# One add on GpSimd in place of one identity product on TensorE, ahead of each finish of an attention and expert layer

## The reference, cut to what matters

```python
x = x + _L0_xattn_ref(_layernorm(x), ctx, ctx, mask, wq, bq, wk, bk, wv, bv, wo, bo)
x = x + _L0_ffn_ref(_layernorm(x), ...)

# _L0_ffn_ref
scores = sigmoid(xf @ gate_w + bias)
top_scores, top_idx = top_k(scores, 2)           # two experts for each token
top_scores = top_scores / (sum(top_scores) + 1e-06)
combined = sum over the two experts of weight * 0.1 * expert(xf)
shared = (gelu(xf @ sw_up + sb_up) @ sw_down + sb_down) * 0.1
out = shared + combined
out = out / (max(abs(out), axis=-1, keepdims=True) + 1e-06)
```

## Time and profile before

| | |
|---|---|
| median of 3 runs | 904.52 us (900.25 to 906.15) |
| the profiled execution | 901.51 us, its span 899.8 us |
| TensorE busy | 819.6 us (91%) |
| VectorE busy | 640.1 us (71%) |
| ScalarE busy | 652.6 us (73%) |
| GpSimd busy | 533.0 us (59%) |
| mean granted clock of TensorE | 0.971 |

### The profile page before, as it was taken

The page is one execution under the profiler, slowest core; times in us unless marked ns, Lnnn a source line. Parts: engine busy times, 40 slices in busy tenths (PEclk is TensorE's granted clock), DMA queues, the critical chain, the costliest instruction groups (busy, mean ns, idle before and its releaser), DMA issues.

```text
span 899.8 us, 21793 instructions
## 1 busy us (share of the span) xinstructions
PE 819.6 (91%) x7037; PEld 552.8 (61%) x7037; DVE 640.1 (71%) x1768; ACT 652.6 (73%) x1184; POOL 533.0 (59%) x631
## 2 busy tenths in 40 slices
PE   0779999998989989999987889999999999999997
PEld 0335555554545545555555667787888888778664
DVE  4355768866768677875756786877777777777677
ACT  1357888887867858677679878987888887889420
POOL 6246555788796857858647772365666565665000
PEclk9889999999989989999989899999999999999999
DMA  5133343442442312222001145566677688851875
GB/s 163 60 110 101 95 129 105 136 126 84 141 134 65 87 42 78 68 63 70 29 13 39 62 158 194 216 232 245 251 245 254 233 294 270 281 198 50 230 209 171
DMA packets 101382, 128.84 MB, mean 143 GB/s; under 512 B 21143, under 2 KB 81367, under 8 KB 95255
## 3 DMA queue, kind: packets, MB, share of 16 engines
q1 hardware_dynamic: 92183, 108.04, 37.4%
q0 software_dynamic: 9088, 19.42, 6.2%
HBM read 78.79 MB, written 40.56 MB: 133 GB/s over the span
## 4 chain that ended last, share of the span: by engine, by line
PE 55%; POOL 20%; issue 11%; ACT 6%; DVE 5%; DMA 2%; SPq 0%; POOLq 0%; ACTq 0%; DVEq 0%
PE bank L1250 7%; POOL xs_scratch L1118 7%; POOL y_scratch L1125 7%; PE bank L1236 5%; ACT prob L708 4%; PE bank L1267 3%; PE bank L1343 3%; PE bank L1342 3%; PE bank L1341 3%; PE bank L1255 3%; PE bank L1330 3%; PE bank L1332 3%; PE bank L1331 3%; POOL prob L1103 2%; PE bank L1229 2%
## 5 line engine op out<-in xcount | busy, mean ns | idle before, releaser
L708 ACT ACTIVATE prob<-bank,padb,sc 120x512 f32<-120x512 f32 x256 | 178.3, 777 | 77.7 <-PE bank L1255 77.7
L1125 POOL DMA_INDIRECT y_scratch<-yo,ti x156 | 158.0, 1013 | 122.6 <-DVE yo L1038 86.6
L1103 POOL TENSOR_SCALAR_AFFINE_SELECT prob<-prob 120x512 f32<-120x512 f32 x256 | 158.6, 634 | 89.7 <-ACT prob L708 85.6
L814 DVE TENSOR_REDUCE nm<-bank 128x4 f32<-128x480 f32 x256 | 150.4, 649 | 80.6 <-PE bank L1236 80.1
L1017 DVE TENSOR_TENSOR gl<-gf,gh 128x512 fp32r<-128x512 f32 x220 | 150.2, 688 | 49.6 <-ACT gh L754 48.9
L1118 POOL DMA_INDIRECT xs_scratch<-x2r,idx x128 | 127.2, 994 | 34.8 <-issue 34.4
L754 ACT ACTIVATE gh<-gf 128x512 fp32r<-128x512 f32 x220 | 138.5, 630 | 5.1
L1250 PE MATMUL bank<-qblk,kT 32*120 32x512 f32 x512 | 111.7, 646 | 3.4 <-DVE nm L814 3.4
L749 ACT ACTIVATE gf<-bank,wt 128x512 f32<-128x512 f32 x156 | 105.9, 679 | 5.3 <-DVE gl L1017 5.1
L1267 PE MATMUL bank<-prob,vm 120*32 120x128 f32 x2048 | 72.8, 285 | 8.9 <-POOL prob L1103 8.8
L1236 PE MATMUL bank<-kblk,qT 32*128 32x480 f32 x512 | 74.0, 646 | 1.5 <-DMA kblk<-kT 1.5
(11 more groups left out here) (190 smaller groups left out, 1654.8 us busy)
## 6 DMA issues: line engine op xcount, KB each, us to landing
wt<-w_scratch SPq DMA_DIRECT2D x39, 1032.0 KB, 5.1
xt<-xs_scratch SPq DMA_DIRECT2D x39, 280.0 KB, 5.0
w_scratch<-x2t SPq DMA_DIRECT2D x8, 1024.0 KB, 5.1
xs_scratch<-padc SPq DMA_DIRECT2D x15, 280.0 KB, 3.0
x<-in_x SPq DMA_DIRECT2D x16, 256.0 KB, 2.9
qblk<-qT SPq DMA_DIRECT2D x64, 64.0 KB, 2.1
x_scratch<-x SPq DMA_DIRECT2D x16, 256.0 KB, 2.9
fx<-x_scratch SPq DMA_DIRECT2D x16, 256.0 KB, 5.4
```

The costliest lines, as they stand in the source:

```text
L708: e.activation(prob[u % NP][0:LK, :], banks[bi][0:LK, :], ACT.Exp, scale=sc[0:LK, 0:1], bias=padb[0:LK, t:t + 1]).then_inc(a_ex, 1)
L814: e.tensor_reduce(nm[:, g, i // 2, :], bk[:, 0:480].rearrange("p (j k) -> p j k", j=4), AX.X, ALU.max, negate=True).then_inc(v_mx, 1)
L1103: e.affine_select(out=pv, in_=pv, compare_op=ALU.is_ge, fill=0.0, base=0, pattern=[[0, 4], [1, 128]], channel_multiplier=-1).then_inc(p_cu ...
L1125: e.indirect_dma_start(y_dram, bass.IndirectOffsetOnAxis(ap=ti_[r % NWS][:, c:c + 1], axis=0), yo_[r % NYO][:, c, :], None).then_inc(d_y[r ...
```

## The change

A stage "fsum" is put into the plan, 2.2 ahead of the finish. In it GpSimd waits for both loads of routed results, adds `fb` to `fa` in place and counts up a new semaphore `p_fs`. TensorE's "sum" waits for `p_fs` where it waited for the loads, and has one identity product, by `fa`, in place of two.

```diff
         plan.append((load, len(plan), "f_load", f, 0))
+        plan.append((time - 2.2, len(plan), "fsum", f, 0))
         plan.append((time - .4, len(plan), "sum", f, 0))
...
+                elif stage == "fsum":
+                    e.wait_ge(d_f[n % NF], 32 * (n // NF + 1))
+                    e.tensor_tensor(fa_[n % NF][:, :, :], fa_[n % NF][:, :, :], fb_[n % NF][:, :, :], ALU.add).then_inc(p_fs, 1)
...
                     e.wait_ge(v_ye, FINS[n] + 1)
-                    e.wait_ge(d_f[n % NF], 32 * (n // NF + 1))
+                    e.wait_ge(p_fs, n + 1)
                     e.matmul(bk[:, :], ident, fa_[n % NF][:, :, :].rearrange("p b h -> p (b h)"), start=True, stop=False, skip_group_check=True)
-                    e.matmul(bk[:, :], ident, fb_[n % NF][:, :, :].rearrange("p b h -> p (b h)"), start=False, stop=False, skip_group_check=True)
                     for b in range(GB):
```

More of the change, by code:

```diff
@@ L471, in xattn_moe_kernel @@
         d_out = [sem(f"d_out{i}") for i in range(NFX)]
-        p_set, p_vz, p_kb, p_qb, p_rs1, p_rs2, p_xb, p_cut, p_wl = map(
-            sem, ("p_set", "p_vz", "p_kb", "p_qb", "p_rs1", "p_rs2", "p_xb", "p_cut", "p_wl"))
+        p_set, p_vz, p_kb, p_qb, p_rs1, p_rs2, p_xb, p_cut, p_wl, p_fs = map(
+            sem, ("p_set", "p_vz", "p_kb", "p_qb", "p_rs1", "p_rs2", "p_xb", "p_cut", "p_wl", "p_fs"))
         v_set, v_id, v_bob, v_km, v_vis, v_poi = map(sem, ("v_set", "v_id", "v_bob", "v_km", "v_vis", "v_poi"))
```

## The result

The changed kernel took 897.6 us (median of 22 runs, 892.4 to 904.1), the kernel before 901.7 us beside it (22 runs, 895.6 to 907.0). The ratio is 0.9957, 95% interval 0.9938 to 0.9977: 3.9 us faster, between 2.1 and 5.6. I had forecast 898 and a gain of 5.9, in a range that ran from 893.4 to 901.5 before it was rounded outwards.

A forecast was written before the change was run, and what follows sets the result against it. TensorE was taken to bound the last 60 us by a third of a microsecond per finish. Ceiling 8.1 us, cut by late loads to 5.9 (4.5 to 7 at 0.54): 895.6 or 898.6, given as 898; range 893.4 to 901.5, rounded outwards.

The forecast's parts named there:

- rival (b): Transfers slower than 2.55 us, or adds sometimes meeting the small TENSOR_SCALAR: 2.86 to 3.1 per step, gain 3 to 4.3; 0.14 shared.
- (d): TensorE's clock drops to 1.2 GHz, a sum then takes 3.5 us: 1 to 2 us lost; chance 0.14 shared.
- What bounds, and what the product is worth: TensorE bounds the last 60 us; one identity product less saves 0.86 us per sum, 2.61 to 1.75.
- The wait in front of sum 0: 1.3: At the start TensorE waits for GpSimd's first add, hidden by nothing: costs 1.3 us, bounds 1.1 and 1.6.
- Mixed half: Sums 0 to 7, among shared tiles' products: step 5.4 to 4.55 us, 5.6 us ahead at its end.
- VectorE's finish at 2.3: Sums 8 to 15: VectorE bounds at 2.3 us against 2.61, gaining 2.5; with the earlier sums a ceiling of 8.1.
- Load 10 late, by SyncE's own chain: SyncE's queue waits on output landings, so finish 10's loads land at about 872.7; one microsecond lost.
- Then finish 10 at 875.9: After load 10: 1.4 us for the add, 1.75 for the sum, 0.05, so finish 10 starts at 875.9.
- At 315 three transfers are 2.5 us ... I take 2.55.: Finishes 10 to 15: the queue's three transfers set 2.55 us per step, 12.8 in all, last finish at 888.7.
- The shared reads: GpSimd's add could hold the finish's small TENSOR_SCALAR; costed at nothing, up to 7.6 us for adds 10 to 15.
- Rival (a): VectorE is the bound and the loads are in time: gain 8.1 us, 893.4; chance 0.20.
- rival (c): Every GpSimd add holds VectorE fully, 1.27 us per finish: 8.5 us slower, 910.0; chance 0.05.

The follow-up runs named there:

- wait_only: Changed kernel with the second identity product put back on TensorE, keeping the wait and GpSimd's add; ratio to the kernel before 1.0036, tail 72.4 us.
- before_mates: Kernel before with late x loads one finish later, 1e-6 added with a PSUM operand, two buffers for maxima and reciprocals; ratio to it 0.9989, tail 69.2 us.
- late_fx: Changed kernel with the five late loads of x one finish later in SyncE's list, behind the next output; ratio to the kernel before 0.9963, tail 65.2 us.
- first_direct: Changed kernel with finish 0 done the old way, both products on TensorE, GpSimd adding from finish 1 on; ratio to the kernel before 0.9945, tail 65.3 us.
- late_and_first: Changed kernel with finish 0 done the old way and the late x loads one finish later; ratio to the kernel before 0.9943, tail 63.6 us.
- filler: Changed kernel with idle identity products on TensorE ahead of its waits in sums 0 (two) and 10 (three); ratio to the kernel before 0.9957, tail 65.4 us.
- combo: Changed kernel with finish 0 the old way, late x loads one finish later, 1e-6 with a PSUM operand, two buffers for maxima and reciprocals; ratio 0.9922, tail 59.9 us.
- after_2: Changed kernel run again, unedited, on another chip; ratio to the kernel before 0.9992, tail 66.0 us.
- eps_psum: Changed kernel with the 1e-6 added by an operation that has one operand in PSUM; ratio to the kernel before 0.9960, tail 67.0 us.

## Why the prediction was right

The time came out (898 against 897.6), and the direction and the order of the gain. The 5.9 was half as large again as the 3.9 measured (4.1 in the profile), and both lie outside the 4.5 to 7 of the forecast. They lie in rival (b), a gain of 3 to 4.3, to which I gave 0.14 together with (d). That the time agrees to half a microsecond is luck: the kernel before, with more runs, has a median of 901.7 and not 904.5, which made up for the gain that was 2 too large. Point by point, by its own steps:

- **What bounds, and what the product is worth.** Right. TensorE's sum fell from 2.61 to 1.75 and the mixed half from 5.4 to 4.54 per finish. wait_only shows that the product is the gain, before_mates that TensorE was the bound.
- **The wait in front of sum 0: 1.3.** Measured 1.38 (0.14 to 1.52 behind the landing). Not foreseen: the clock can fall there, which cost 1.7 more in wait_only and late_fx.
- **Mixed half, 5.6 ahead at its end.** Finish 7 starts 37.7 us into the tail against 43.5 before, 5.9, of which 0.3 is a quicker first landing. VectorE was held there (0.96 and 0.52, and in the remainders) and a single step was 5.0, but the next gave it back; finish 5 still waits for TensorE.
- **VectorE's finish at 2.3.** Undersized. It is 2.40: with no wait for TensorE in between, the end of one finish must be seen before the next begins, and that takes 0.13 and not 0.03. The ceiling was therefore 5.6 + 8 x 0.21 = 7.3, not 8.1.
- **Load 10 late, by SyncE's own chain.** Right. Landing forecast at 872.7, the add began at 872.89; first_direct against late_and_first shows the chain to be the cause.
- **Then finish 10 at 875.9.** It was 877.49. The sum behind the wait ran at the low clock: 3.17 and not 1.75. I had this as rival (d) but reasoned from a busy share of 69% over the whole half, and did not look at the one place where TensorE would stand for 3 us. filler shows the 1.2 to 1.8 us. The price that (d) named, 1 to 2, was right.
- **"At 315 three transfers are 2.5 us ... I take 2.55."** This step failed as a step between finishes: steps 12 to 15 are 2.40, VectorE's own, and combo runs at 2.16 over the same traffic. As a pace of loads it was not far off. The adds of finishes 10 to 15 begin 2.78 us apart in the mean in the changed kernel (872.89 to 886.81), 2.36 to 2.55 in after_2, eps_psum, filler and first_direct. What I missed is that a pace bounds only when no stock is left. In combo add 10 begins 8.9 us before its finish and add 15 still 4.5. In the changed kernel there was no stock at finish 10; the low clock and the hold there let the loads get ahead again, by so little that finish 14 had 0.05 us of room and finish 15 0.2. So rival (b) at 2.86 per step (890.2 for the last finish, measured 890.45) described the loads of this execution well.
- **The shared reads: "I cost it at nothing".** Failed too. The add of finish 12 began at 878.05, because the load was late again, just ahead of the small TENSOR_SCALAR, and held it for 0.95. The alignment that I worked out belonged to a pace that did not come about. The Trainium skill, SBUF — State Buffer, "Practical consequences", was the better guide: between a VectorE instruction in a two-port mode and one of GpSimd, whoever issues first has the shared ports for its whole instruction, and the other is blocked. The traces agree: in four places above the held instruction ends within 0.03 us of the end of the add. The same list says that a VectorE instruction with at most one input in SBUF, outside the two-port modes, does not contend with GpSimd. eps_psum, where one of the two inputs is in PSUM, agrees: 157 to 159 ns in all 16.

The sum from finish 7 on: finish 10 1.6 later (with it the two steps before that were 0.1 longer), the step to finish 11 0.8 longer than 2.55, the last four 0.15 shorter: 1.8 us less than forecast. That is the 5.9 against the 4.1 of the profile. These are the steps as they ran, not what each cause would give back alone: without the low clock and the hold, the loads of this execution would have kept the end within 0.1 us of where it was.

Rival (a) named the right bound for the steps and had the wrong price; (b) and (d) together had the time and what happened, slower loads, one meeting of an add with the small TENSOR_SCALAR on the path and one sum at the low clock; rival (c) had the right mechanism at one finish where it wanted all.

## What to carry to other kernels

When one engine bounds by a third of a microsecond per step, taking 0.86 off it buys the third and whatever lies in stretches where the others have room. The rest has to be bought from the next engine and from the queue behind it, by edits that measured as nothing before: here three of them and a direct first finish turned 4 us into 9.5 to 9.8 of the tail. Look for the queue's waits on its own landings before reckoning with its bandwidth, look beside the chain for what was ready only just in time, and after moving work to GpSimd list what VectorE does with SBUF operands only.

## What the runs showed of the hardware

- A GpSimd add of 128x512 f32 (1.27 us in the median) holds a four-column TENSOR_SCALAR of VectorE between SBUF operands to its end, up to 1.26 us in all (filler) where it takes 0.17 alone; the same with one operand in PSUM takes 0.158 us beside it. It goes the other way too: 1.73 us for one add in the changed kernel, 2.38 in late_fx, beside VectorE's subtractions of two SBUF operands.
- TensorE that stood for 2.8 to 4.4 us in front of sum 10 ran afterwards at 0.50 to 0.60 of its clock in the mean of the next 3.2 to 3.4 us, in five profiles of five. In front of sum 0, where it stood for 1.85 to 2.02 us, that came in 2 of 5 profiles (0.59 in wait_only, 0.52 in late_fx). Behind 1.94 us in filler and 2.27 us in front of sum 14 of the changed kernel it stayed at 1.00. A mean of 0.6 is a stretch at both levels, 1.2 and 2.4 GHz, mostly the lower.
- VectorE starts an operation 0.13 us behind the end of the four-piece update on which it waits, and 0.08 ahead of it (0.34 to 0.35 per piece, overlapped) if it need not: 2.39 against 2.16 per finish.
